# First attention of an eight-sublayer kernel: head maxima of the first two groups in eight PSUM banks, later batches projected between maxima, layer norms cut into pieces

## The chip, the cores and the metric

One Trainium2 chip, one of its cores. The core has five engines that run their own instruction streams and wait for each other by semaphores: TensorE (PE in the profile; its weight loads are PEld), VectorE (DVE), ScalarE (ACT), GpSimd (POOL) and SyncE (SP), which here issues transfers. The metric is the device time of one launch in microseconds (us); less is better.

## The reference

The input `x` has 4 sequences of 512 tokens of 128 features. Eight sublayers follow, each `x = x + f(layernorm(x))`: attention A, experts, attention B, experts, then four more of another kind. The change touches the first sublayer, attention A, and the layer norm of the second. Attention A is causal softmax attention with 16 heads of 8 features. The reference goes over key blocks with a running maximum, which is the same as subtracting each row's maximum over all allowed keys:

```python
def proj(W):
    y = jnp.einsum('btm,nm->btn', x, W)
    return y.reshape(Bx, Tx, N_HEADS, D_HEAD).transpose(0, 2, 1, 3)
Q, K, V = (proj(Wq), proj(Wk), proj(Wv))
...
scores = scale * jnp.einsum('bhtd,bhsd->bhts', Q, kb)
scores = jnp.where(future[None, None], -jnp.inf, scores)
m_new = jnp.maximum(m, jnp.max(scores, axis=-1, keepdims=True))
p = jnp.exp(scores - m_new)
...
return acc / jnp.maximum(l, 1e-12)
```

The layer norm ahead of each sublayer is `(x - m) / jnp.sqrt(v + 1e-5)` over the 128 features.

## The kernel before

Every engine has a function of its own for each sublayer, and the order of its calls, written out by hand, is the order of that engine's instructions. Nothing is reordered afterwards. PSUM is used as eight banks of 128 x 512 f32 (`bank(M, b)`); `take` makes PE wait until the last reader of a bank is done.

**The work of attention A.** A batch is one sequence (four, b = 0 to 3). A group n is four heads of one batch, so there are 16 groups and n // 4 is the batch. For each group the kernel does the following. *Maxima*: PE computes the scores of a 128-row tile of queries against the keys up to it, adds the causal mask by one more matmul, and DVE reduces them to a row maximum (`maxima`/`reduce`, 11 jobs of 384 or 512 columns a group, in the two side banks 6 and 7 in turn). *Split and rows*: DVE splits the maxima into three bf16 parts (`maxima_split`), PE transposes them (`rows`), DVE copies them (`row_copy`) and SP puts them as extra rows beside the queries, so that the second pass of scores comes out with the maximum subtracted. *Exps*: PE computes the transposed scores (`exps`, `tail`), ACT takes the exponential into `a_PT`, GpSimd zeroes what the mask forbids (`seen`). *Values*: PE multiplies them with the values and with a column of ones (`values`), ACT copies the result (`evict`), PE turns it (`turned`), and DVE divides (`normalize`). In the loop over n = 2 to 15, PE works on the maxima of group n + 2, the exponentials of group n and the values of group n - 1, woven together.

**Where queries and keys come from.** For groups 2 to 15 PE projects a batch (`factor`, q and k), ACT copies the result to `a_f`, which is split into three bf16 parts of `a_parts` by four steps (`split`: cast, subtract, cast, subtract) on GpSimd, except the keys of batch 0, which DVE splits. SP writes the parts to HBM (`write`) and reads them back spread over partitions (`read(n)`). A `read(n)` is 0.58 MB in four transfers, and those of groups 4 to 7 wait until batch 1 is written. Groups 0 and 1 of batch 0 are handled without that trip: PE projects them anew in a layout with one head in each block of 32 partitions (`own`), and their maxima (`own_maxima`, `own_reduce`), rows (`own_rows`, `own_add`) and exponentials (`own_exps`) use f32 matmuls on 32 rows, four heads at a time. The maxima of such a group come in three parts, by tiles of queries: `A_FIRST = [[3], [0, 2], [1]]`, of 512, 128 + 384 and 256 columns a head. They use banks 4 to 7, one a head, so that a part's matmuls wait until DVE has reduced the part before.

**The norms.** `norm_front` (DVE: statistics of four tiles, their aggregates, the variance), `norm_root` (GpSimd: the power -1/2), `norm_back` (DVE: one Newton step of four small operations, then four scalings into `XN`), then PE's `turn_tensor` and ACT's `turn_scalar` into `XNT`. Norm 0 is that of attention A; all four batches' fronts are at the start, and the backs of batches 1, 2 and 3 stand among the first maxima. Norm 1 is that of the experts: batch b - 1 gets its residual in group n = 4b + 2 (n = 6, 10, 14), and its norm follows there and in the next group. `expert_bias` is a preparation for the experts on DVE, in the group n = 14.

## Time and profile before

| | |
|---|---|
| median of 3 runs | 1227.47 us (1222.32 to 1230.30) |
| profiled execution: its time, its span | 1233.54 us, 1231.8 us |
| attention A in the span | 0 to about 250 us |
| busy in the whole span | PE 81%, DVE 68%, ACT 32%, POOL 28% |
| mean granted TensorE clock | 0.875 of full |

The profile is of one execution. A timeline row gives start, length, engine, line and operation, what it writes and reads, the count of instructions merged, and in brackets the idle time of the engine before it with what ended it; a "+" of neighbours on one line is merged, so a row can hold short waits. The granted clock of TensorE is 1.00 (2.4 GHz) or 0.50 (1.2 GHz); values between are stretches with both.

### The profile page before, as it was taken

The page shows a single profiled execution, that of the slowest core. Times are in us where ns is not written, and L with a number is a line of the kernel's source. Part 1 is how long each engine was busy: PE and PEld are TensorE (multiplying, and loading weights), DVE is VectorE, ACT ScalarE, POOL GpSimd, SP SyncE. Part 2 cuts the span into 40 slices and gives each one's busy share as a digit, 9 for nine tenths or more (in the row PEclk, how much of TensorE's full clock was granted, in tenths as well). Part 3 has the DMA queues.
Part 4 walks back from the last instruction along what each step waited for, and adds up shares of the span by engine and source line. Part 5 has one row for each costly group of instructions (what it writes and reads, how often), then busy time and mean ns, then how long its engine had stood idle before and what let it go on. Part 6 is the DMA issues. An engine that isn't in the chain of part 4 may idle for free.

```text
span 1231.8 us, 16801 instructions
## 1 busy us (share of the span) xinstructions
PE 1001.3 (81%) x6199; PEld 589.5 (48%) x6199; DVE 838.8 (68%) x1999; ACT 388.7 (32%) x650; POOL 345.2 (28%) x350
## 2 busy tenths in 40 slices
PE   6799899789999877699789754999999565997475
PEld 3334444334343655444334322766777344776244
DVE  7578787566554567766765476747655996588895
ACT  2335454523433243323323262221212122331121
POOL 5442222212233443212222303022020343232232
PEclk9889898989999687889889886999999796887786
DMA  5532121020000000000000000000000000000000
GB/s 136 146 104 60 40 60 61 32 89 1 1 1 1 1 1 1 1 0 1 1 0 1 1 0 3 1 1 1 1 1 1 1 1 1 2 2 2 0 10 26
DMA packets 11534, 24.35 MB, mean 20 GB/s; under 512 B 1323, under 2 KB 7635, under 8 KB 11315
## 3 DMA queue, kind: packets, MB, share of 16 engines
q1 hardware_dynamic: 11152, 22.28, 6.1%
...
## 4 chain that ended last, share of the span: by engine, by line
PE 55%; DVE 32%; issue 6%; ACT 3%; POOL 2%; DMA 1%; DVEq 0%; ACTq 0%; SPq 0%; POOLq 0%
PE ps L880 5%; PE ps L867 4%; PE ps L872 4%; PE ps L308 3%; PE ps L258 3%; DVE a_MN L462 2%; DVE XN L117 2%; DVE q_E L1501 2%; PE ps L1701 2%; PE ps L1762 2%; PE ps L1716 2%; PE ps L1759 2%; PE ps L278 2%; PE ps L2292 2%; DVE g_C L1637 1%
## 5 line engine op out<-in xcount | busy, mean ns | idle before, releaser
L1124 POOL TENSOR_TENSOR f_Y<-f_Y,f_TT 128x512 f32<-128x512 f32 x56 | 70.9, 1266 | 181.0 <-DVE f_TT L1014 181.0
L462 DVE TENSOR_REDUCE a_MN<-ps 128x1 f32<-128x384 f32 (+3 forms) x154 | 94.9, 639 | 35.0 <-PE ps L261 33.2
L1089 ACT ACTIVATE f_HH<-ps,pack_zero 128x512 f32<-128x512 f32 x64 | 44.0, 688 | 135.3 <-PE ps L867 135.2
L96 POOL TENSOR_TENSOR rs<-t,mhalf 128x4 f32<-128x4 f32 x37 | 37.5, 1015 | 175.3 <-DVE t L90 175.1
L143 DVE TENSOR_TENSOR X<-ps,X 128x512 f32<-128x512 f32 x32 | 22.0, 688 | 93.9 <-PE ps L1772 49.5
L597 ACT ACTIVATE a_PT<-ps 128x1024 f32<-128x1024 f32 x56 | 57.4, 1025 | 75.1 <-PE ps L278 73.9
L880 PE MATMUL ps<-f_HH,pack_zero 128*128 128x512 f32 x128 | 75.5, 673 | 5.7 <-DVE f_TT L1014 5.7
L1005 DVE TENSOR_TENSOR f_XS<-ps,XNT 128x512 f32<-128x512 f32 x64 | 43.9, 689 | 51.6 <-PE ps L860 51.5
L867 PE MATMUL ps<-f_XS,pack_zero 128*128 128x512 f32 x128 | 70.7, 636 | 1.1 <-DVE f_XS L1005 1.1
L258 PE MATMUL ps<-a_KS,a_QS 72*128 72x128 bf16 (+3 forms) x224 | 59.5, 326 | 13.1 <-DVE a_MN L462 7.5
L1014 DVE SCALAR_TENSOR_TENSOR f_TT<-ps,pack_zero,f_X 128x512 f32<-128x512 f32 x64 | 47.9, 748 | 32.0 <-PE ps L880 31.9
L872 PE MATMUL ps<-f_XS,pack_zero 128*128 128x512 f32 x128 | 68.7, 619 | 0.0
L2115 PE MATMUL ps<-pack_one,XNT 128*128 128x352 f32 x128 | 49.9, 538 | 22.6 <-DVE q_HH L2164 22.3
L688 POOL TENSOR_SCALAR_AFFINE_SELECT a_PT<-a_PT 128x256 f32<-128x256 f32 x64 | 26.0, 407 | 119.0 <-ACT a_PT L597 111.2
L2134 PE MATMUL ps<-pack_one,q_HT 128*128 128x128 f32 (+1 forms) x192 | 36.1, 334 | 20.9 <-ACT q_HT L2217 20.9
L308 PE MATMUL ps<-a_PT,a_VA 128*32 128x128 f32 (+3 forms) x512 | 51.1, 472 | 2.2 <-POOL a_PT L691 2.1
L258 PEld LDWEIGHTS ps<-a_KS,a_QS 72*128 72x128 bf16 x224 | 19.1, 102 | 62.6 <-DVE a_MN L462 41.5
L1093 ACT ACTIVATE f_X<-ps 128x512 f32<-128x512 f32 x64 | 38.2, 597 | 32.8 <-PE ps L873 32.8
L2115 PEld LDWEIGHTS ps<-pack_one,XNT 128*128 128x128 f32 x128 | 27.2, 225 | 40.3 <-DVE q_HH L2164 26.6
L278 PE MATMUL ps<-a_QS,a_KS 75*128 75x512 bf16 (+1 forms) x224 | 46.3, 313 | 0.0
L2134 PEld LDWEIGHTS ps<-pack_one,q_HT 128*128 128x128 f32 (+1 forms) x192 | 29.3, 228 | 30.2 <-ACT q_HT L2217 23.2
L1959 POOL TENSOR_TENSOR h_RN<-h_N,mhalf 128x32 f32<-128x32 f32 x4 | 21.7, 5433 | 76.3 <-DVE h_N L1818 76.3
...
## 6 DMA issues: line engine op xcount, KB each, us to landing
...
X<-in_x SPq DMA_DIRECT2D x4, 256.0 KB, 10.1
...
a_QS<-a_MT SPq DMA_DIRECT2D x42, 4.0 KB
```

Source lines behind the costliest of these rows:

```text
L258: pe.matmul(bank(M, bk, N, N * u), M.a_QS[0:72, i, h, 128 * ti:128 * ti + 128], M.a_KS[0:72, i, h, 0:N], start=(u == 0), stop=False, skip_ ...
L278: return pe.matmul(out, M.a_KS[0:75, i, h, 128 * si:128 * si + 128], M.a_QS[0:75, i, h, 128 * si:512], start=True, stop=True)
L308: m = pe.matmul(bank(M, 5, N, 128 * si, 32 * j, 32 * j + 32), M.a_VA[:, i, si, 4 * g + j, :], M.a_PT[:, (4 * n + j) % 8, A_AT[si]:A_AT[si] ...
L462: dve.tensor_reduce(M.a_MN[:, n % 2, ti, h0:h0 + k], bank(M, M.bank["a_max", n, jj], 128 * (ti + 1) * k).rearrange("p (a c) -> p a c", a=k ...
L597: act.activation(M.a_PT[:, c % 8, 0:1024], M.ps[:, a * 512:a * 512 + 1024], ACT.Exp).then_inc(made.sem, made.tick(n, hh))
L867: pe.matmul(bank(M, 2 + u % 2), M.f_w1[:, e, :], M.f_XS[:, x, :], start=True, stop=True).then_inc(made.sem, made.tick(n, u, 1))
L872: pe.matmul(bank(M, 4), M.f_w3[:, e, :], M.f_XS[:, x, :], start=True, stop=False)
L880: pe.matmul(bank(M, 5), M.f_w2[:, e, :], M.f_HH[:, u % 3, :], start=True, stop=True).then_inc(made.sem, made.tick(n, u))
L1014: dve.scalar_tensor_tensor(M.f_TT[:, u % 3, :], bank(M, 5), M.f_b2[:, e:e + 1], M.f_X3[:, u % 3, :], ALU.add, ALU.mult).then_inc(made.sem, ...
L1124: pool.tensor_tensor(M.f_Y[:, i, :], M.f_Y[:, i, :], M.f_TT[:, u % 3, :], ALU.add).then_inc(made.sem, made.tick(n, u))
L2115: pe.matmul(bank(M, 2 * k + s, 352), M.XNT[:, 128 * t:128 * t + 128], M.WG[:, s, :], start=True, stop=True).then_inc(made.sem, made.tick(n ...
L2134: m = pe.matmul(bank(M, bo, 128, 128 * (t % 4)), M.q_HT[0:rows, t % 2, a, :], M.WD[0:rows, a, :], start=(a == 0), stop=(a == 2))
```

## The change

- The first maxima: `own_maxima` gets the first bank and the number of heads that it takes at a time. Group 0 puts its first part in banks 4 to 7, its second in banks 0 to 3, its third in banks 4 to 7 two heads at a time; group 1 uses banks 4 to 7, the later two parts two heads at a time.
- What stood among these maxima is moved behind them: `own(1)` behind the rows of group 0, batch 1's turning and `factor` behind the maxima of group 1, `plain(0)` behind that; batch 2's turning and `factor` stand between the maxima of group 2, batch 3's between those of group 3. ACT, DVE and GpSimd follow the same order.
- Batch 0's keys are split on GpSimd, ahead of batch 1's, and no longer on DVE.
- DVE: all twelve `own_reduce` of group 0 come first, then `own_add`, then norm 0's back of batch 1; those of batches 2 and 3 come behind group 1's rows and behind `reduce(3, 1)`.
- Norm 1 of batches 0 to 2 is cut up: statistics, aggregates, Newton step and scalings stand between the reduces of the group with g = 3, one group boundary later than before. GpSimd's root for it stands ahead of that group's `seen` instead of behind the previous group's, which is the same place in its own order.

```diff
-    own_maxima(0, 0)
-    own(1, "q", 1)
-    own(1, "k", 2)
-    plain(0, 3)
-    own_maxima(0, 1)
+    own_maxima(0, 0, 4, 4)
+    own_maxima(0, 1, 0, 4)
+    own_maxima(0, 2, 4, 2)
+    own_rows(0, 6)
+    own(1, "q", 4)
+    own(1, "k", 5)
+    own_exps(0, 0)
+    own_maxima(1, 0, 4, 4)
+    own_exps(0, 1)
+    own_maxima(1, 1, 4, 2)
+    own_exps(0, 2)
+    own_maxima(1, 2, 4, 2)
     turn_tensor(pe, S, M, 0, 1, 0, M.XN, (S["normed"], (0, 1)))
+    own_rows(1, 4)
     factor(1, "q", 1)
     factor(1, "k", 2)
-    own_maxima(0, 2)
-    own_rows(0, 3)
-    own_exps(0, 0)
-    own_maxima(1, 0)
...
+    plain(0, 3)
     pe.wait_ge(S["in_ones"].sem, 16)
     own_exps(1, 0)
-    for jj in range(4):
+    maxima(2, 0)
+    maxima(2, 1)
+    turn_tensor(pe, S, M, 0, 2, 4, M.XN, (S["normed"], (0, 2)))
+    maxima(2, 2)
+    maxima(2, 3)
+    factor(2, "q", 4)
+    maxima(2, 4)
+    factor(2, "k", 5)
+    own_exps(1, 1)
+    for jj in range(5, 9):
         maxima(2, jj)
     values(0, 0)
...
     values(0, 3)
+    maxima(3, 1)
     turn_tensor(pe, S, M, 0, 3, 0, M.XN, (S["normed"], (0, 3)))
+    maxima(3, 2)
+    maxima(3, 3)
     factor(3, "q", 1)
+    maxima(3, 4)
     factor(3, "k", 2)
+    maxima(3, 5)
+    rows(2)
     plain(1, 3)
```

```diff
     for n in range(2, 16):
         b, g, more = n // 4, n % 4, n + 2 < 16
-        if more:
-            for jj in range(5):
+        left = b - 1 if g == 3 and b else None
+        for jj in range(5):
+            if more:
                 reduce(n + 2, jj)
+            if left is not None and jj < 2:
+                norm_stats(dve, S, M, left, M.X, range(2 * jj, 2 * jj + 2))
+            if left is not None and jj == 2:
+                norm_mean(dve, S, M, 1, left)
         if n + 1 < 16:
             row_copy(n + 1)
         if more:
             reduce(n + 2, 5)
-        if g == 3 and b:
-            norm_back(dve, S, M, 1, b - 1, M.X, M.XN)
+        if left is not None:
+            norm_refine(dve, S, M, 1, left)
+        if more:
+            reduce(n + 2, 6)
+        if left is not None:
+            norm_scale(dve, S, M, 1, left, M.X, M.XN, range(0, 2))
         normalize(n - 2)
...
-        if g == 2 and b:
-            norm_front(dve, S, M, 1, b - 1, M.X)
         if n == 14:
             expert_bias(dve, S, M)
```

```diff
     for b in range(4):
         norm_root(pool, S, M, 0, b)
-    split(0, "q")
-    split(1, "q")
-    split(1, "k")
+    for b in range(2):
+        split(b, "q")
+        split(b, "k")
```

**PE at the start.** L208 and L215 (after: L229 and L236) are the first maxima and their mask, `a_QS` holding the queries and keys of groups 0 and 1; L185/L204 is `own(1)`, L193 `plain`, L127 the turning, L177 `factor`, L226/L247 `own_rows`, L262 `own_exps`. Before, from the first maxima of group 0 to its rows:

```order
L208 MATMUL ps<-a_QS 128x512 x4
L215 MATMUL ps<-pack_half 128x128 x4
L185 MATMUL ps<-XNT,pack_first 128x512 x2
L193 MATMUL ps<-pack_first,XNT 128x128 x4
L208 MATMUL ps<-a_QS 128x128 x4
L208 MATMUL ps<-a_QS 128x384 x4
L215 MATMUL ps<-pack_half 128x2x128 x4
L127 MATMUL ps<-pack_first,XN 128x128 x4
L177 MATMUL ps<-XNT,pack_first 128x512 x2
L208 MATMUL ps<-a_QS 128x256 x4
L215 MATMUL ps<-pack_half 128x128 x4
L226 MATMUL ps<-pack_first,a_OL 128x128 x4
```

The same stretch of the change:

```order
L229 MATMUL ps<-a_QS 128x512 x4
L236 MATMUL ps<-pack_half 128x128 x4
L229 MATMUL ps<-a_QS 128x128 x4
L229 MATMUL ps<-a_QS 128x384 x4
L236 MATMUL ps<-pack_half 128x2x128 x4
L229 MATMUL ps<-a_QS 128x256 x2
L236 MATMUL ps<-pack_half 128x128 x2
L229 MATMUL ps<-a_QS 128x256 x2
L236 MATMUL ps<-pack_half 128x128 x2
L247 MATMUL ps<-pack_first,a_OL 128x128 x4
L204 MATMUL ps<-XNT,pack_first 128x512 x2
```

Between the first maxima and the rows of group 0 nothing is left but maxima; the projections and the turning stand behind.

**DVE at the boundary of group n = 6 and in group n = 7.** L462/L478 is a reduce, L85/L84 to L90/L94 the front of norm 1 for batch 0, L101 (L110) the first step of its back, L477/L493 the last step of a maxima split, L484/L500 `row_copy`. Before, from the end of the split in group 6:

```order
L477 TENSOR_TENSOR a_M<-a_MR,a_M 128x4x4
L85 BN_STATS st<-X 128x6 x4
L88 BN_AGGR mv<-st 128x2 x4
L90 TENSOR_SCALAR t<-mv 128x4
L462 TENSOR_REDUCE a_MN<-ps 128x4
L462 TENSOR_REDUCE a_MN<-ps 128x2 x2
L462 TENSOR_REDUCE a_MN<-ps 128x1 x2
L484 COPY a_MT<-ps 12x512
L462 TENSOR_REDUCE a_MN<-ps 128x1
L101 TENSOR_TENSOR t<-rs 128x4
```

The same stretch of the change:

```order
L493 TENSOR_TENSOR a_M<-a_MR,a_M 128x4x4
L478 TENSOR_REDUCE a_MN<-ps 128x4
L84 BN_STATS st<-X 128x6 x2
L478 TENSOR_REDUCE a_MN<-ps 128x2
L84 BN_STATS st<-X 128x6 x2
L478 TENSOR_REDUCE a_MN<-ps 128x2
L92 BN_AGGR mv<-st 128x2 x4
L94 TENSOR_SCALAR t<-mv 128x4
L478 TENSOR_REDUCE a_MN<-ps 128x1 x2
L500 COPY a_MT<-ps 12x512
L478 TENSOR_REDUCE a_MN<-ps 128x1
L110 TENSOR_TENSOR t<-rs 128x4
```

The front stood in one piece ahead of the first reduce; it is now between the first four reduces. Of the back, which follows, the diff shows that one reduce now comes ahead of the scalings, and that two of them stand behind the division.

**DVE at the end of the loop, n = 14 and 15**, where no maxima are left. L819/L839 is the end of `expert_bias`. Before:

```order
L85 BN_STATS st<-X 128x6 x4
L88 BN_AGGR mv<-st 128x2 x4
L90 TENSOR_SCALAR t<-mv 128x4
L805 CAST f_hb<-pack_zero 48x128
L807 TENSOR_TENSOR f_r<-pack_zero,f_hb 48x128
L809 CAST f_mb<-f_r 48x128
L811 TENSOR_TENSOR f_r<-f_r,f_mb 48x128
L812 TENSOR_SCALAR f_hi<-f_hb,pack_zero 48x128
L814 SCALAR_TENSOR_TENSOR f_mid<-f_mb,pack_zero,f_hi 48x128
L816 SCALAR_TENSOR_TENSOR f_r<-f_r,pack_zero,f_mid 48x128
L819 TENSOR_SCALAR f_B<-f_r,pack_zero 48x128 x8
L101 TENSOR_TENSOR t<-rs 128x4
```

The same stretch of the change:

```order
L836 SCALAR_TENSOR_TENSOR f_r<-f_r,pack_zero,f_mid 48x128
L839 TENSOR_SCALAR f_B<-f_r,pack_zero 48x128 x8
L84 BN_STATS st<-X 128x6 x4
L92 BN_AGGR mv<-st 128x2 x4
L94 TENSOR_SCALAR t<-mv 128x4
L110 TENSOR_TENSOR t<-rs 128x4
L112 TENSOR_TENSOR t<-t 128x4
L114 TENSOR_SCALAR t<-t 128x4
L116 TENSOR_TENSOR rs<-rs,t 128x4
```

The statistics of batch 2 stood ahead of `expert_bias`, with GpSimd's root beside it; they are now behind it, directly ahead of the Newton step.

## Rows read from the trace of the kernel before

**Rows 1.** The profile page: span; the chain that ended last, by engine

```profile
span 1231.8 us, 16801 instructions
...
PE 55%; DVE 32%; issue 6%; ACT 3%; POOL 2%; DMA 1%; DVEq 0%; ACTq 0%; SPq 0%; POOLq 0%
```

**Rows 2.** The chain of waits that ended last: start, length, what

```profile
28.00 2.65 DVE XN L117 x3
```

**Rows 3.** Timeline of the first maxima on PE and DVE, and GpSimd's splits beside them

```profile
14.53 1.14 PE L208 MATMUL ps<-a_QS 32*128 32x512 f32 x8
...
15.80 2.92 DVE L117 TENSOR_SCALAR XN<-X,mv,rs 128x128 f32<-128x128 f32 x4
...
18.64 2.47 DVE L448 TENSOR_REDUCE a_OL<-ps 128x1 f32<-128x512 f32 x4
...
23.27 2.74 DVE L448 TENSOR_REDUCE a_OL<-ps 128x1 f32<-128x128 f32 x8
...
26.14 0.61 POOL L673 CAST a_parts<-a_f 128x512 bf16<-128x512 f32 x1 [6.27 <-ACT a_f L571]
...
27.01 3.64 DVE L117 TENSOR_SCALAR XN<-X,mv,rs 128x128 f32<-128x128 f32 x4
...
32.12 1.09 PE L226 MATMUL ps<-pack_first,a_OL 128*128 128x128 f32 x4 [4.82 <-DVE a_OL L448]
...
32.56 1.15 POOL L679 TENSOR_TENSOR a_parts<-a_rest,a_parts 128x512 bf16<-128x512 f32 x1
...
34.20 2.09 PE L241 MATMUL ps<-a_QS 32*128 32x512 f32 x8 [0.99 <-DVE a_QS L456]
```

**Rows 4.** Timeline: one `factor` of q and k; `read(4)`; first exponentials of groups 2 and 3

```profile
24.28 1.96 PE L177 MATMUL ps<-XNT,pack_first 128*128 128x512 f32 x4 [0.78 <-ACT XNT L135]
...
39.84 0.31 SPq L723 DMA_DIRECT2D a_QS<-scratch  x1
...
76.31 1.06 PE L278 MATMUL ps<-a_QS,a_KS 75*128 75x512 bf16 x3
...
88.48 0.60 PE L278 MATMUL ps<-a_QS,a_KS 75*128 75x512 bf16 x3
```

**Rows 5.** Stretches: length, busy PE, PEld, DVE, ACT, POOL (instructions), granted clock, DMA share, GB/s

```profile
20.00:22.00 2.00, 0.63 (x13) 0.56 (x16) 1.97 (x4) 0.00 (x0) 0.00 (x0) 1.00 0.59 198
...
30.00:32.00 2.00, 0.00 (x0) 0.00 (x0) 1.98 (x5) 0.00 (x0) 1.86 (x3) 0.59 0.88 195
...
71.70:81.40 9.70, 9.50 (x39) 3.09 (x37) 6.54 (x15) 1.02 (x1) 3.02 (x4) 0.50 0.50 165
```

**Rows 6.** The same view over four stretches from one group's values to the next's

```profile
88.50:98.60 10.10, 9.70 (x85) 4.26 (x84) 8.68 (x20) 5.58 (x9) 2.95 (x7) 1.00 0.22 72
...
132.30:148.20 15.90, 12.70 (x92) 5.82 (x95) 12.61 (x39) 6.61 (x9) 3.88 (x7) 0.84 0.14 38
...
148.20:159.00 10.80, 10.40 (x84) 4.29 (x83) 8.02 (x18) 5.25 (x8) 2.93 (x6) 0.92 0.22 57
...
182.00:198.80 16.80, 13.67 (x91) 6.16 (x87) 12.38 (x38) 6.34 (x9) 3.89 (x7) 0.76 0.16 56
```

**Rows 7.** Timeline of group 7: norm front, GpSimd's root, PE's two waits for DVE

```profile
132.56 0.86 DVE L85 BATCH_NORM_STATS2 st<-X 128x6 f32<-128x128 f32 x4
...
133.99 1.01 POOL L96 TENSOR_TENSOR rs<-t,mhalf 128x4 f32<-128x4 f32 x1 [1.80 <-DVE t L90]
...
134.56 0.39 PE L258 MATMUL ps<-a_KS,a_QS 72*128 72x256 bf16 x2 [1.15 <-DVE a_MN L462]
...
140.91 0.39 PE L258 MATMUL ps<-a_KS,a_QS 72*128 72x512 bf16 x1 [1.68 <-DVE a_f L497]
```

**Rows 8.** Timeline of groups 14 and 15 on DVE and PE

```profile
230.56 2.20 DVE L819 TENSOR_SCALAR f_B<-f_r,pack_zero 48x128 bf16<-48x128 f32 x8
...
233.47 1.32 DVE L117 TENSOR_SCALAR XN<-X,mv,rs 128x128 f32<-128x128 f32 x4
...
237.39 2.36 PE L308 MATMUL ps<-a_PT,a_VA 128*32 128x512 f32 x32
```

More of the change, by code:

```diff
@@ L447, in own_reduce @@
             N = 128 * (ti + 1)
-            m = dve.tensor_reduce(M.a_MX[:, n, ti, 32 * j + 8:32 * j + 9], bank(M, 4 + j, N, at), AXX, ALU.max, negate=True)
+            m = dve.tensor_reduce(M.a_MX[:, n, ti, 32 * j + 8:32 * j + 9], bank(M, M.bank["a_max", n, part, j], N, at), AXX, ALU.max, negate=True)
             at += N
@@ L505, in attn_a_vector @@
         norm_front(dve, S, M, 0, b, M.X)
+    for part in range(3):
+        for j in range(4):
+            own_reduce(0, part, j)
+    own_add(0)
     norm_back(dve, S, M, 0, 1, M.X, M.XN)
-    for j in range(4):
-        own_reduce(0, 0, j)
-    split("k")
-    for j in range(4):
-        own_reduce(0, 1, j)
-    norm_back(dve, S, M, 0, 2, M.X, M.XN)
-    for j in range(4):
-        own_reduce(0, 2, j)
-    own_add(0)
     for part in range(3):
@@ L523, in attn_a_vector @@
     maxima_split(2)
-    for jj in range(6):
+    reduce(3, 0)
+    reduce(3, 1)
+    norm_back(dve, S, M, 0, 3, M.X, M.XN)
+    for jj in range(2, 6):
         reduce(3, jj)
@@ L538, in attn_a_vector @@
             reduce(n + 2, 5)
-        if g == 3 and b:
-            norm_back(dve, S, M, 1, b - 1, M.X, M.XN)
+        if left is not None:
[4 more added lines that the diff above has]
+            norm_scale(dve, S, M, 1, left, M.X, M.XN, range(0, 2))
         normalize(n - 2)
         if more:
-            for jj in range(6, 9):
-                reduce(n + 2, jj)
+            reduce(n + 2, 7)
+        if left is not None:
+            norm_scale(dve, S, M, 1, left, M.X, M.XN, range(2, 4))
+        if more:
+            reduce(n + 2, 8)
         if g == 2 and b:
@@ L547, in attn_a_vector @@
         if more:
-            for jj in range(9, 11):
-                reduce(n + 2, jj)
+            reduce(n + 2, 9)
+            reduce(n + 2, 10)
             maxima_split(n + 2)
-        if g == 2 and b:
-            norm_front(dve, S, M, 1, b - 1, M.X)
         if n == 14:
@@ L633, in attn_a_scalar @@
     own(1)
-    plain(0)
+    for part in range(3):
+        own_exps(0, part)
     turn_scalar(act, S, M, 0, 1)
     factors(1)
-    for part in range(3):
-        own_exps(0, part)
+    plain(0)
+    own_exps(1, 0)
     turn_scalar(act, S, M, 0, 2)
     factors(2)
-    for part in range(3):
-        own_exps(1, part)
+    own_exps(1, 1)
+    own_exps(1, 2)
     turn_scalar(act, S, M, 0, 3)
```

112 lines of the change are left out of this document (48 added, 64 removed).

## Prediction

> **What bounds the kernel now.** I read the page first: the span, and the chain that ended last, which is 55% PE and 32% DVE [rows 1]. No engine is full; the two hand work to each other, so a microsecond counts where one waits for the other. Attention A is some 250 us of the span and the only part that the change touches, so I went through it by the chain of waits, the timeline and stretches with the granted clock. Three places matter.
>
> *The start.* The first maxima run at 14.53, and group 0's exponentials start only at 34.20 [rows 3]. DVE is what they wait for: batch 1's norm back (2.92), four reduces (2.47), the keys' split, eight reduces (2.74), batch 2's norm back (3.64), and then the last four. The second norm back is in the chain of waits [rows 2], and PE stands still 4.82 us until 32.12 for what follows it [rows 3]. The clock falls in that gap: the stretch 30 to 32 has 0.59, while 20 to 22, after a shorter gap, has 1.00 [rows 5]. Group 2's exponentials come at 76.31, in a cold stretch (0.50 from 71.7 to 81.4, PE busy 9.50 of 9.70), and group 3's at 88.48 [rows 4, 5]. A warm group takes 10.10 with PE busy 9.70: PE sets that pace, DVE has 1.4 to spare [rows 6].
>
> *Groups 7 and 11.* They hold norm 1 and take 15.90 and 16.80, with DVE busy 12.61 and 12.38 and a mean clock of 0.84 and 0.76; the group behind the first takes 10.80 [rows 6]. PE waits 1.15 for the front and 1.68 for the back [rows 7], and then the clock falls.
>
> *The end.* In groups 14 and 15 DVE does `expert_bias` to 232.76, then the last norm back to 234.79; PE's turning, ACT's copy and the last values (237.39) follow [rows 8].
>
> **The change, part by part.** The sum is made against the profiled 1233.5 us. The median is 6.1 lower, 1227.5; I carry the difference over.
>
> *A. To group 0's exponentials.* DVE's first reduce can start when mask and fronts are done, about 15.8, where the old norm back started. Now nothing is between the reduces: 2.47 + 2.74 + 1.47 (from 30.65, the end of the norm back, to PE's 32.12) = 6.7, to 22.5. PE always has the next part ready, since the second is in free banks and the third needs only four reduces. The rows and the addition took 2.08 (32.12 to 34.20) at the low clock; with the 1.09 of transposes halved it is 1.5. PE meanwhile does `own(1)`, as large as the `factor` of 1.96 [rows 4]: 22.5 + 0.7 + 2.0 = 25.2 is the start of the exponentials, against 34.20: 9.0 less.
>
> *B. From there to group 2's exponentials.* Group 1's maxima start at 26.4 behind 1.1 of exponentials' matmuls. Their twelve reduces again cost 6.7, plus 0.4 where PE waits for ACT to give banks back: 27.8 to 34.8. Then on PE rows 0.7, `factor` 2.0, `plain` 1.0 (half of `factor`'s), hand-over and ACT's copy 0.9: 39.5. One part of exponentials, and DVE's first reduce of group 2 comes at 41.2. Group 2's eleven maxima would take 7; `factor(2)`, two parts of exponentials and two of values stand between them on PE and make it 12, to 53.2. DVE's split 1.0, two reduces 1.3 (2.47 is four), batch 3's norm back 2.0 (232.76 to 234.79 in [rows 8]): 57.5. Turning and ACT's copy 1.3, nine reduces, the row copy and the waits for `factor(3)` 7.6: 66.4. So group 2's exponentials start at 66.5 instead of 76.31: **9.8 less**. Before, this way held less of projections (they lay under DVE's work), which is why it gains hardly more than A.
>
> *What the move puts elsewhere.* Batch 0's key split leaves DVE and costs GpSimd one split: two took 26.14 to 33.71, so 3.8 [rows 3]. It ends at 23.7, where DVE's was done before 23.27, so group 2's copies from HBM come no later. Batch 1's splits now start at 37.5 rather than 26.1; GpSimd then has splits, `seen(0)` (3.0, GpSimd's 2.95 of a group [rows 6]), splits, `seen(1)`, splits in a row. `seen(0)` ends at 48.1, and PE wants it at 48.8: covered by 0.7. SP's `read(4)` to `read(7)` wait for the write of batch 1 and go at 47.7 instead of 39.84 [rows 4]; 2.3 MB at the 165 GB/s of a stretch full of writes [rows 5] are 14 us, so the last lands by 62, and PE asks for the first at 66. The norm backs of batches 1 and 2 lie where DVE waits for PE anyway (from 24.1 and from 36.4; the latter may be stretched like the 2.92 and 3.64 by GpSimd's splits, to 40): nothing.
>
> *C. The group after.* From group 2's exponentials to group 3's took 12.17 [rows 4], a warm group 10.10 [rows 6]: 5.1 of cold clock cost 2.1. **2.1 less** if it is warm.
>
> *D. The price of new gaps.* PE is idle 19.0 to 22.6 (its maxima are done, DVE is not) and 55.0 to 57.5 (for batch 3's norm back). The old gap of 4.82 brought the clock down, the one ahead of 21.37 (2.7) did not; 3.6 and 2.5 are between and below. A fall costs something like the 2.1 of C; with the chain half on DVE, I take 0 to 3 each and **2.5 more** for one of two.
>
> Here the skill speaks against the change. The Trainium skill, "TensorE: Matmul & The Clock Gate", section "HAM oscillation — how this bites in real kernels", says that a matmul stream with waits between its bursts is throttled again at each and starts every burst cold, and reckons the penalty at half of the throttled time. By it the 5.1 us of C would cost 2.55, where the rows have 2.1. No row shows whether a gap of 3.6 brings a fall.
>
> *E. Groups 7 and 11.* DVE's work is the same, 12.6; only its order changes. Its front is 1.43 from statistics to the root's start [rows 7]. In pieces, PE's first wait of 1.15 becomes waits of 0.45, 0.25 and 0.4 behind each piece. The long one stays: PE wants the side bank that `normalize` frees, and ahead of that DVE had Newton step, four scalings and division, and has now Newton step, a reduce, two scalings and division. Two scalings are exchanged for one reduce, 0.6 each, so the 1.68 stays. From DVE's split to its next, counted through, it is 13.1 after 13.2: as good as nothing at the same clock. What can be had is the cold clock: a group of 14.0 instead of 15.90 and 16.80, and 10.1 instead of 10.8 behind it: 2.6 and 3.5. PE's idle time falls from 3.2 (15.90 less 12.70) to about 2.5 a group, so I take it for one of the two: **3 less**. The ends are +0.5 (more small waits, nothing warm) and 6.1 less.
>
> *F. The end.* In n = 14 the statistics stood ahead of `expert_bias` and GpSimd's root beside it. Now all is in a row: `expert_bias` ends 1.3 earlier, at 231.5, then 1.43 of front, 1.0 of root, 0.1 of hand-over, 0.7 of Newton step, and 1.3 of scalings with a division of 0.7 between them: 236.7 instead of 234.79. PE turns, ACT copies and only then evicts group 14, so the last values move from 237.39 to 239.3: **1.9 more**. GpSimd's root also stands ahead of group 15's `seen`, which ends at 237.1 and is covered. From here everything is serial and moves along.
>
> Sum: -9.8 - 2.1 + 2.5 - 3.0 + 1.9 = -10.5: 1223 for a profiled run, **1217** for the median.
>
> **The rivals.** *All warm.* No new gap brings the clock down, and both norm groups keep it: -9.8 - 2.1 - 6.1 + 1.9 = -16.1, **1211**. For it: the 2.7 gap did not matter. Against: the 1.68 wait stays, and both such groups have a mean clock well below 1.
>
> *Cold as ever.* The rule of the skill cited above: both gaps of the start cost 2.5, and the norm groups gain nothing: -9.8 - 2.1 + 5 + 0.5 + 1.9 = -4.5, **1223**. For it: PE's bursts at the start are about 3 us between waits.
>
> *The start is held by GpSimd and the transfers.* Batch 1's splits are 11 later and their user is 10 earlier; the margins are 0.7 for `seen(0)` and a few us for the reads. If `seen` is slower beside DVE, or the transfers are, the group 2 chain stands at about 73: 3 instead of 9.8 won, **1224**. In the extreme, the change does not do what it says: 1227.
>
> *Slower.* The clock falls in the first new gap and, as small gaps follow each other, does not rise before group 2's exponentials. In 71.7 to 81.4 it stayed low 9.7 us with PE busy 98%, so work alone does not raise it at once. PE has about 27 of warm work between 22.6 and 66.5, 54 when cold, in 44: more than 10 late, which eats A and B, and F stays: **1230**. It decides from some 30 us of unbroken cold; that stretch of 9.7 is the longest that I can point to.
>
> **How the numbers follow.** Chances: forecast 0.39, all warm 0.24, cold as ever 0.23, GpSimd and transfers 0.10, slower 0.04. About 1%, 12.3 us, is what a measurement of this kernel can tell from no change; the three runs before lie 8 apart. Faster by more than 1% means below 1215.2: nearly all of the warm case and a quarter of the forecast's own, 1212 to 1221, make 0.33; slower by over 1% 0.02; the rest 0.65. The range takes in the warm and the cold case with their bounds: 1209 to 1226.
>
> **What the changed profile would show.** Group 0's first exponentials' matmuls at 25 (A); group 2's at 66 to 69 (B); group 3's 10.1 behind (C); the granted clock in 20 to 24 and 56 to 62 (D); group 7 at 14 or at 16, with PE's wait of 1.7 behind the division in both (E); DVE's last scalings ahead of the last values later than `expert_bias` by 5, not by 2 (F). I am wrong if group 2's maxima wait for their copies, if GpSimd ends `seen(0)` after PE asks for it, or if the clock stays up in the norm groups although the wait remains.

## The result, and the profile after

| | before | changed |
|---|---|---|
| median (range) | 1228.88 us (1222.32 to 1231.57), 4 runs | 1247.86 us (1246.15 to 1251.64), 4 runs |
| profiled execution, its span | 1233.54, 1231.8 | 1251.64, 1249.8 |
| mean granted clock | 0.875 | 0.864 |

The ratio is 1.0167, with a 95% interval of 1.0119 to 1.0214. It is estimated from all runs of both kernels, so it is not exactly the quotient of the two medians. The whole interval is above 1: the kernel is slower, and the forecast of 1217 was wrong in sign.

The two lines of the page that say most are those of the costliest groups for DVE's reduces and PE's maxima. In the kernel before they are:

```profile
L462 DVE TENSOR_REDUCE a_MN<-ps 128x1 f32<-128x384 f32 (+3 forms) x154 | 94.9, 639 | 35.0 <-PE ps L261 33.2
...
L258 PE MATMUL ps<-a_KS,a_QS 72*128 72x128 bf16 (+3 forms) x224 | 59.5, 326 | 13.1 <-DVE a_MN L462 7.5
```

The page of the changed kernel:

```profile
span 1249.8 us, 16805 instructions
...
PE 58%; DVE 30%; issue 6%; ACT 3%; POOL 2%; DMA 0%; DVEq 0%; ACTq 0%; POOLq 0%
...
L478 DVE TENSOR_REDUCE a_MN<-ps 128x1 f32<-128x384 f32 (+3 forms) x154 | 95.0, 640 | 48.5 <-PE ps L282 47.9
...
L279 PE MATMUL ps<-a_KS,a_QS 72*128 72x128 bf16 (+3 forms) x224 | 60.3, 330 | 19.4 <-DVE a_f L513 12.4
```

The reduces are as many and as long as before (154, 95 us), but DVE now waits 48.5 us ahead of them instead of 35.0. PE waits 19.4 us ahead of its maxima instead of 13.1, and the first cause has changed: not a reduce (`a_MN`) but `a_f` of L513, the last step of the division in `normalize`. Nothing in the forecast accounts for that.

One warm group without a norm shows why. Stretches of the changed kernel, with the columns of [rows 5]:

```profile
98.20:109.30 11.10, 9.79 (x83) 4.23 (x83) 8.72 (x20) 5.53 (x8) 2.94 (x6) 1.00 0.42 103
...
133.50:151.20 17.70, 14.93 (x97) 6.63 (x97) 13.05 (x40) 7.04 (x10) 4.35 (x8) 0.76 0.13 32
```

The first is such a group, at full clock: 11.10 instead of 10.10 [rows 6], with the same work for PE (9.79 and 9.70) and DVE (8.72 and 8.68). The second is group 7 with 0.7 of the group ahead of it, at a mean clock of 0.76. The middle of the first, in the timeline, is:

```profile
101.54 0.41 DVE L500 COPY a_MT<-ps 12x512 bf16<-12x512 bf16 x1
...
102.45 0.56 DVE L478 TENSOR_REDUCE a_MN<-ps 128x1 f32<-128x384 f32 x1 [0.49 <-PE ps L282]
...
103.06 0.34 PE L279 MATMUL ps<-a_KS,a_QS 72*128 72x384 bf16 x1 [0.21 <-DVE a_MN L478]
...
103.49 0.56 DVE L478 TENSOR_REDUCE a_MN<-ps 128x1 f32<-128x384 f32 x1 [0.49 <-PE ps L282]
...
103.97 0.16 DVE L509 TENSOR_SCALAR a_RS<-ps 128x16 f32<-128x16 f32 x1
...
104.45 0.29 DVE L513 TENSOR_TENSOR a_f<-ps,a_RS 128x128 f32<-128x128 f32 x1
...
104.80 0.39 PE L279 MATMUL ps<-a_KS,a_QS 72*128 72x512 bf16 x1 [0.91 <-DVE a_f L513]
```

The same place in the kernel before:

```profile
93.66 0.56 DVE L462 TENSOR_REDUCE a_MN<-ps 128x1 f32<-128x384 f32 x1 [0.49 <-PE ps L261]
...
94.14 0.16 DVE L493 TENSOR_SCALAR a_RS<-ps 128x16 f32<-128x16 f32 x1
...
94.62 0.29 DVE L497 TENSOR_TENSOR a_f<-ps,a_RS 128x128 f32<-128x128 f32 x1
94.83 1.32 DVE L462 TENSOR_REDUCE a_MN<-ps 128x1 f32<-128x384 f32 x2
...
94.97 0.39 PE L258 MATMUL ps<-a_KS,a_QS 72*128 72x512 bf16 x1
```

PE's job 7 of the maxima (the first of 512 columns) needs the side bank that the division frees. Before, DVE divided directly behind its reduce of job 5, while PE computed job 6. Now `reduce(n + 2, 6)` stands ahead of `normalize(n - 2)`, so DVE first waits 0.49 for job 6's matmuls, then reduces them, then divides. From the reduce of job 5 to PE's job 7 it takes 104.80 - 102.45 = 2.35 instead of 94.97 - 93.66 = 1.31: **1.04 more in a group**. The diff has this swap outside every condition on `left`; it holds in all twelve groups that have maxima to reduce (n = 2 to 13), not only in the two of them with a norm.

**Where the time went.** The two profiled executions, stage by stage:

| stretch | before | changed | difference |
|---|---|---|---|
| group 2's exponentials start | 76.31 | 70.68 | -5.6 |
| values of group 1 start | 77.94 | 72.08 | -5.9 |
| from there, groups 2 to 13 | 142.00 | 156.21 | +14.2, of it 12 x 1.04 = 12.5 |
| groups 14 and 15 | 17.45 | 22.07 | +4.6, of it 3.25 in the last |
| the last values start | 237.39 | 250.36 | +13.0 |
| batch 3's scalings of norm 1 | 249.15 | 265.31 | +16.2 |
| span | 1231.8 | 1249.8 | +18.0 |

The last values' 32 matmuls alone took 2.36 [rows 8] before and 4.50 now, at the low clock; that is 2.1 of the 3.2 between the last values and batch 3's scalings. I call the start of those scalings **the mark** below: it ends attention A, and no kernel here changes anything behind it.

**The end**, in the timeline of the changed kernel:

```profile
239.23 1.65 DVE L839 TENSOR_SCALAR f_B<-f_r,pack_zero 48x128 bf16<-48x128 f32 x8
...
242.36 1.01 POOL L105 TENSOR_TENSOR rs<-t,mhalf 128x4 f32<-128x4 f32 x1 [4.00 <-DVE t L94]
...
244.15 0.57 DVE L114 TENSOR_SCALAR t<-t 128x4 f32<-128x4 f32 x1
...
245.11 0.99 DVE L131 TENSOR_SCALAR XN<-X,mv,rs 128x128 f32<-128x128 f32 x2
...
246.71 0.60 DVE L131 TENSOR_SCALAR XN<-X,mv,rs 128x128 f32<-128x128 f32 x2
247.45 0.63 PE L146 MATMUL ps<-pack_first,XN 128*128 128x128 f32 x4 [3.64 <-DVE XN L131]
...
250.36 4.50 PE L329 MATMUL ps<-a_PT,a_VA 128*32 128x512 f32 x32
```

PE stands still 3.64 us for the scalings, and the clock is down when the last values start.

**The start.** Stretches of the changed kernel around its two new gaps, and PE's and DVE's rows there:

```profile
20.00:22.00 2.00, 0.00 (x0) 0.00 (x0) 2.00 (x7) 0.00 (x0) 1.85 (x3) 1.00 0.33 107
22.00:24.00 2.00, 1.24 (x5) 0.92 (x6) 1.06 (x3) 0.00 (x0) 1.86 (x3) 0.78 1.03 342
24.00:26.00 2.00, 2.00 (x4) 0.67 (x2) 1.86 (x9) 0.69 (x1) 0.24 (x1) 0.50 0.86 288
...
58.00:60.00 2.00, 0.00 (x0) 0.00 (x0) 1.90 (x5) 0.00 (x0) 2.00 (x5) 0.50 0.78 174
```

```profile
22.76 0.76 PE L247 MATMUL ps<-pack_first,a_OL 128*128 128x128 f32 x4 [3.06 <-DVE a_OL L464]
23.31 3.49 PE L204 MATMUL ps<-XNT,pack_first 128*128 128x512 f32 x4
26.73 1.14 PE L262 MATMUL ps<-a_QS 32*128 32x512 f32 x8
...
54.37 1.04 DVE L487 CAST a_M<-a_MN 128x16 bf16<-128x16 f32 x1
...
58.24 0.57 DVE L114 TENSOR_SCALAR t<-t 128x4 f32<-128x4 f32 x1
...
59.20 1.50 DVE L131 TENSOR_SCALAR XN<-X,mv,rs 128x128 f32<-128x128 f32 x4
60.84 1.09 PE L146 MATMUL ps<-pack_first,XN 128*128 128x128 f32 x4 [5.65 <-DVE XN L131]
...
70.68 0.82 PE L299 MATMUL ps<-a_QS,a_KS 75*128 75x512 bf16 x3
```

The clock fell in the second gap and directly behind the first, so twice and not once. Behind the first, `own(1)` took 3.49 instead of about 2.0. The second was 5.65 long, not 2.5.

### The profile page after: what moved, and what is told of

Read it like the earlier page. It is cut to its first block, busy times and chain, and to the rows that moved or that the text cites. A ratio compares the mean times of both kernels' runs of the same rounds, so it can differ in the third digit from the quotient of the medians.

```text
span 1249.8 us, 16805 instructions
## 1 busy us (share of the span) xinstructions
PE 1017.0 (81%) x6199; PEld 603.2 (48%) x6199; DVE 841.8 (67%) x1995; ACT 389.4 (31%) x650; POOL 348.6 (28%) x354
## 4 chain that ended last, share of the span: by engine, by line
PE 58%; DVE 30%; issue 6%; ACT 3%; POOL 2%; DMA 0%; DVEq 0%; ACTq 0%; POOLq 0%
PE ps L900 5%; PE ps L887 4%; PE ps L892 4%; PE ps L329 3%; PE ps L279 3%; DVE a_MN L478 3%; PE ps L2312 2%; PE ps L1782 2%; DVE XN L131 2%; PE ps L1721 2%; PE ps L1736 2%; PE ps L1779 2%; DVE q_E L1521 2%; PE ps L299 1%; DVE g_C L1657 1%
## 5 line engine op out<-in xcount | busy, mean ns | idle before, releaser
L478 DVE TENSOR_REDUCE a_MN<-ps 128x1 f32<-128x384 f32 (+3 forms) x154 | 95.0, 640 | 48.5 <-PE ps L282 47.9
L900 PE MATMUL ps<-f_HH,pack_zero 128*128 128x512 f32 x128 | 73.0, 652 | 5.7 <-DVE f_TT L1034 5.7
L279 PE MATMUL ps<-a_KS,a_QS 72*128 72x128 bf16 (+3 forms) x224 | 60.3, 330 | 19.4 <-DVE a_f L513 12.4
L887 PE MATMUL ps<-f_XS,pack_zero 128*128 128x512 f32 x128 | 68.6, 619 | 1.3 <-DVE f_XS L1025 1.3
L892 PE MATMUL ps<-f_XS,pack_zero 128*128 128x512 f32 x128 | 67.5, 610 | 0.0
L329 PE MATMUL ps<-a_PT,a_VA 128*32 128x128 f32 (+3 forms) x512 | 55.4, 509 | 1.4 <-POOL a_PT L714 1.3
L299 PE MATMUL ps<-a_QS,a_KS 75*128 75x512 bf16 (+1 forms) x224 | 48.8, 326 | 0.1
```

The costliest lines, as they stand in the source:

```text
L279: pe.matmul(bank(M, bk, N, N * u), M.a_QS[0:72, i, h, 128 * ti:128 * ti + 128], M.a_KS[0:72, i, h, 0:N], start=(u == 0), stop=False, skip_ ...
L299: return pe.matmul(out, M.a_KS[0:75, i, h, 128 * si:128 * si + 128], M.a_QS[0:75, i, h, 128 * si:512], start=True, stop=True)
L329: m = pe.matmul(bank(M, 5, N, 128 * si, 32 * j, 32 * j + 32), M.a_VA[:, i, si, 4 * g + j, :], M.a_PT[:, (4 * n + j) % 8, A_AT[si]:A_AT[si] ...
L478: dve.tensor_reduce(M.a_MN[:, n % 2, ti, h0:h0 + k], bank(M, M.bank["a_max", n, jj], 128 * (ti + 1) * k).rearrange("p (a c) -> p a c", a=k ...
L887: pe.matmul(bank(M, 2 + u % 2), M.f_w1[:, e, :], M.f_XS[:, x, :], start=True, stop=True).then_inc(made.sem, made.tick(n, u, 1))
L892: pe.matmul(bank(M, 4), M.f_w3[:, e, :], M.f_XS[:, x, :], start=True, stop=False)
```

## The experiments

"Division" is `normalize(n - 2)`, "job k" is the k-th part of a group's maxima and its reduce. The mark and the group lengths come from one profiled execution each, a group's length being the time from the start of the values of the group ahead of it to that of its own. The ratios are against the kernel before, run beside it on the same chip: its median was 1234.72 beside e1 to e4, 1231.88 beside e5 to e8 and 1230.58 beside e9 and e10.

| kernel | median us | ratio to before, 95% | mark | group 7, group 11, last group |
|---|---|---|---|---|
| before | | | 249.15 | 15.81, 16.92, 8.61 |
| changed | 1247.86 | 1.0167 (1.0119 to 1.0214) | 265.31 | 16.97, 16.27, 11.86 |
| e1_r6_back | 1232.41 | 1.0001 (0.9972 to 1.0031) | 243.56 | 13.02, 15.73, 12.31 |
| e2_r6_only | 1244.89 | 1.0078 (1.0053 to 1.0102) | 266.60 | 17.67, 17.57, 9.08 |
| e3_start_only | 1230.75 | 0.9979 (0.9954 to 1.0003) | 242.76 | 15.95, 17.24, 8.62 |
| e4_pieces_only | 1236.04 | 1.0022 (0.9994 to 1.0050) | 250.75 | 13.02, 15.57, 12.31 |
| e5_end_as_before | 1226.26 | 0.9970 (0.9942 to 0.9997) | 239.59 | 13.02, 16.22, 8.61 |
| e6_divide_first | 1220.01 | 0.9913 (0.9882 to 0.9944) | 237.00 | 12.57, 12.56, 8.61 |
| e7_gap_filled | 1219.56 | 0.9903 (0.9873 to 0.9933) | 234.61 | 12.56, 12.57, 8.61 |
| e8_back3_early | 1216.01 | 0.9870 (0.9843 to 0.9897) | 236.03 | 12.57, 12.56, 8.61 |
| e9_changed_again | 1245.35 | 1.0108 (1.0051 to 1.0165) | 262.24 | 16.94, 16.28, 11.86 |
| e10_before_divide_first | 1233.42 | 1.0030 (0.9998 to 1.0062) | 249.09 | 14.74, 17.59, 10.20 |

**e1: only job 6 put back behind the division**, in all groups; the rest of the change stays.

```diff
-        if more:
-            reduce(n + 2, 6)
         if left is not None:
             norm_scale(dve, S, M, 1, left, M.X, M.XN, range(0, 2))
         normalize(n - 2)
         if more:
+            reduce(n + 2, 6)
             reduce(n + 2, 7)
```

> The changed kernel, but in every group of the loop DVE divides first and reduces job 6 behind it, as before the change. Theory 1 (DVE's division, which frees a side bank for PE, comes later by one reduce in each of the twelve groups with maxima, at 1.0 us a group): the loop goes back to 10.1 us a warm group, 12 us less than the changed kernel, so 0.990 to 0.997 of the kernel before (the start gains 5.6, the end loses 3 to 5, the clock in the last values 2). Theory 2 (the loop is slow because the new start leaves GpSimd, the copies and the clock in another state): it stays at 1.016 and a group at 11.1.

Groups 3, 4 and 13 are back at 10.08, and the slowdown is gone: ratio 1.0001 (0.9972 to 1.0031). The gain of 0.3 to 1% over the kernel before, which I expected as well, did not come. In groups 2 to 13 e1 takes 137.2 where the changed kernel took 156.2 (153.5 in its second profile, e9), 16 to 19 more. So beside the 12.5 that the swap costs directly, the changed kernel lost 4 to 6.5 there, in groups that it ran in part at the low clock and e1 did not. On the page, DVE's wait ahead of its reduces falls from 48.5 to 30.9, PE's ahead of its maxima from 19.4 to 9.6, and the first cause is a reduce again:

```profile
L478 DVE TENSOR_REDUCE a_MN<-ps 128x1 f32<-128x384 f32 (+3 forms) x154 | 94.5, 638 | 30.9 <-PE ps L282 29.5
...
L279 PE MATMUL ps<-a_KS,a_QS 72*128 72x128 bf16 (+3 forms) x224 | 57.8, 317 | 9.6 <-DVE a_MN L478 5.6
```

**e2: only job 6 ahead of the division**, in the kernel before.

```diff
+        if more:
+            reduce(n + 2, 6)
         normalize(n - 2)
         if more:
-            for jj in range(6, 9):
+            for jj in range(7, 9):
                 reduce(n + 2, jj)
```

> The kernel before with one edit: in every group of the loop DVE reduces job 6 ahead of the division, not behind it. Theory 1: a warm group takes 11.1 instead of 10.1 and the whole 12 us more, 1.010 of the kernel before. Theory 2: no change, 0.998 to 1.002.

This one swap costs 0.78% (0.53 to 1.02), 9.6 us, and makes warm groups of 11.13. Groups 2 to 13 take 157.6 instead of 142.0 in its profile, again more than 12.5. Its page has the changed kernel's signature:

```profile
L462 DVE TENSOR_REDUCE a_MN<-ps 128x1 f32<-128x384 f32 (+3 forms) x154 | 95.2, 640 | 49.3 <-PE ps L261 48.5
...
L258 PE MATMUL ps<-a_KS,a_QS 72*128 72x128 bf16 (+3 forms) x224 | 61.0, 333 | 23.0 <-DVE a_f L497 13.4
```

Put in alone, the swap makes the kernel slower by 0.78%; taken out alone, it takes away the 1.08 to 1.67% that the changed kernel loses (e9 and the first comparison). That settles the cause of the sign. The sizes do not quite add up: with the swap out, the rest of the change makes no difference (e1), so the other 0.3 to 0.9% would arise only where both are together; for e9's 1.08% the intervals overlap, and it may be nothing. The traces show such time in groups 7, 8 and 13, which the changed kernel runs in part at the low clock and e1 does not. That this is all of it is not shown.

**e3: the new start with DVE's loop of before**, so that norm 1 is in two pieces at its old places and job 6 behind the division.

```diff
 # DVE, for n in range(2, 16): as before the change
+        if g == 3 and b:
+            norm_back(dve, S, M, 1, b - 1, M.X, M.XN)
         normalize(n - 2)
...
+        if g == 2 and b:
+            norm_front(dve, S, M, 1, b - 1, M.X)
```

> The start of the changed kernel with DVE's loop of the kernel before (norm 1 in one piece at its old place, division ahead of job 6). Theory 1: group 2's exponentials at 70.7 and 10.1 a group from there, so 4 to 6 us less than the kernel before, 0.995 to 0.997. Theory 2: 1.00 or more, since the late splits and copies slow the groups behind them.

Group 2's exponentials start at 70.65, 5.7 earlier than before, and the mark is 6.4 earlier. The median shows 0.2% less (at most 0.46%), which can't be told from nothing.

**e4: the pieces of norm 1 with the old start**, job 6 behind the division.

```diff
 # the kernel before, with DVE's loop of e1:
+            if left is not None and jj < 2:
+                norm_stats(dve, S, M, left, M.X, range(2 * jj, 2 * jj + 2))
+            if left is not None and jj == 2:
+                norm_mean(dve, S, M, 1, left)
```

> The start of the kernel before with the norms of the loop in pieces, the division ahead of job 6. Theory 1: the pieces alone gain nothing in groups 7 and 11 (15.5 to 16 each) and cost 2 to 3 us at the end, where they stand behind the experts' bias: 1.001 to 1.003. If the pieces were what costs, it would be 1.01 or more.

Groups 7, 8, 11 and 12 take 13.02 + 10.08 + 15.57 + 11.56 = 50.2 instead of 15.81 + 10.89 + 16.92 + 11.16 = 54.8, so the pieces gain 4.5 there. The last group takes 12.31 instead of 8.61, which gives 3.7 back, and the last values' 32 matmuls take 3.33 instead of 2.36. The whole can't be told from nothing: +0.22% (-0.06 to +0.50). I had expected 15.5 to 16 for groups 7 and 11; group 11 took that and group 7 did not. PE's three longest waits are the same in both (0.44, 0.33 and 1.17), and so they are in e1 and e5, but in all three kernels group 7 keeps the full clock and group 11 loses it behind the wait of 1.17. Here are both in e5:

```profile
127.00:140.00 13.00, 10.47 (x88) 4.65 (x87) 11.86 (x39) 5.98 (x9) 3.79 (x7) 1.00 0.07 16
...
172.80:189.10 16.30, 14.00 (x92) 6.28 (x95) 12.41 (x39) 6.54 (x9) 3.80 (x7) 0.76 0.18 57
```

**e5: e1 with batch 2's norm as before**, its statistics ahead of `expert_bias` in n = 14 and its back in one piece at n = 15.

```diff
-        left = b - 1 if g == 3 and b else None
+        left = b - 1 if g == 3 and 0 < b < 3 else None
...
+        if n == 15:
+            norm_back(dve, S, M, 1, 2, M.X, M.XN)
         normalize(n - 2)
...
         if n == 14:
+            norm_front(dve, S, M, 1, 2, M.X)
             expert_bias(dve, S, M)
```

> The changed kernel with the division ahead of job 6 (as e1), and with norm 1 of batch 2 as in the kernel before: statistics ahead of the experts' bias in n = 14, one back in n = 15. Theory (the pieces behind the bias delay the last norm, PE's turning, ACT's copy and the last values): from group 14's values to the last ones 8.6 us, not 12.3, and 3.7 us less than e1: 0.996 to 0.998 of the kernel before. Rival (the 12.3 is GpSimd's masks or the clock): it stays at 12.

The last group is 8.61 again, and the mark 4.0 earlier than in e1. The ratio, 0.9970 (0.9942 to 0.9997), is as expected and just clear of 1.

**e6: e5 with the division ahead of the norm's steps** in groups 7 and 11 too, and these further apart.

```diff
             reduce(n + 2, 5)
-        if left is not None:
-            norm_refine(dve, S, M, 1, left)
-            norm_scale(dve, S, M, 1, left, M.X, M.XN, range(0, 2))
         normalize(n - 2)
         if more:
             reduce(n + 2, 6)
+        if left is not None:
+            norm_refine(dve, S, M, 1, left)
+        if more:
             reduce(n + 2, 7)
         if left is not None:
-            norm_scale(dve, S, M, 1, left, M.X, M.XN, range(2, 4))
+            norm_scale(dve, S, M, 1, left, M.X, M.XN, range(0, 2))
         if more:
             reduce(n + 2, 8)
+        if left is not None:
+            norm_scale(dve, S, M, 1, left, M.X, M.XN, range(2, 4))
```

> As e5, and in groups 7 and 11 DVE divides directly behind job 5, ahead of the Newton step, whose result is needed only at the group's end. Theory (PE's wait of 1.6 is for the side bank that the division frees): the wait goes, both groups take about 12.5 us at full clock, 0.5 to 3 us each less than in e5. Rival (DVE's 12.6 of work sets the group whatever the order): no change, 13.0.

Both groups take 12.6 at full clock, and groups 3, 4, 8, 12 and 13 their warm 10.08. The stretches of groups 7 and 11 in e6:

```profile
126.80:139.40 12.60, 10.69 (x88) 4.66 (x87) 11.54 (x39) 6.09 (x9) 3.79 (x7) 1.00 0.08 21
172.20:184.80 12.60, 10.69 (x88) 4.66 (x87) 11.54 (x39) 6.10 (x9) 3.80 (x7) 1.00 0.22 74
```

PE's longest wait is now 0.46 in both. The ratio is 0.9913, and the whole interval is below 1. The edit moved the division forward and the norm's steps apart at once; which of the two did how much was not tried.

**e7: e6 with `own(1)` ahead of group 0's rows on PE**, in banks 0 and 1, to fill the first gap. **e8: e7 with batch 3's norm 0 back behind `reduce(2, 4)`**, to take it out of the second gap.

```diff
 # e7, PE
-    own_rows(0, 6)
-    own(1, "q", 4)
-    own(1, "k", 5)
+    own(1, "q", 0)
+    own(1, "k", 1)
+    own_rows(0, 6)
 # e8, DVE
-    for jj in range(11):
+    for jj in range(5):
+        reduce(2, jj)
+    norm_back(dve, S, M, 0, 3, M.X, M.XN)
+    for jj in range(5, 11):
         reduce(2, jj)
     maxima_split(2)
-    reduce(3, 0)
-    reduce(3, 1)
-    norm_back(dve, S, M, 0, 3, M.X, M.XN)
```

> As e6, and the projections of group 1 stand ahead of group 0's rows on PE, in banks 0 and 1, where PE otherwise stands still 3 us. Theory (the clock fell in that gap, and the projections were on the way to the exponentials): the clock stays at 1.00 to 28, group 0's exponentials start at 24.5, not 26.7, and 2 us less stay to the end. Rival (DVE and GpSimd set the pace behind it): earlier there, but nothing left at group 2's exponentials.

> As e7, and norm 0's back of batch 3 stands on DVE behind job 4 of group 2, where DVE waits for PE, and not behind job 1 of group 3. Theory (PE's idle 5.7 us ahead of batch 3's turning, with the clock falling in it, is the largest loss of the new start): the idle goes and group 2's exponentials come 4 to 6 us earlier, at 64 to 66. Rival (group 2 then waits for GpSimd, for its mask of group 1 or for copies): 1 or less.

In e7 the gap ahead of the rows shrank from 3.06 to 1.28, and group 0's exponentials started at 24.23 instead of 27.22. The clock still fell, later:

```profile
22.00:24.00 2.00, 0.63 (x4) 0.42 (x4) 1.19 (x4) 0.26 (x1) 1.85 (x3) 1.00 1.02 342
24.00:26.00 2.00, 1.77 (x12) 1.09 (x16) 1.86 (x9) 0.29 (x1) 0.32 (x1) 0.71 0.84 291
26.00:28.00 2.00, 2.00 (x16) 0.39 (x8) 0.35 (x2) 1.78 (x4) 0.00 (x0) 0.50 0.32 81
```

The mark moved 2.4, the median not measurably. The expected full clock up to 28 did not come. e8's profiled execution began its maxima 2.2 later than e7's (its `own(1)` starts at 21.68 instead of 19.50), and even so group 2's exponentials came 1.1 earlier (67.69 for 68.80), so the step itself gained 3.3, less than the 4 to 6 expected. Most of it was lost again at once: the clock was down from 67 to 77, and group 2 took 13.44 instead of 11.27. The mark is 1.4 later than in e7, so without the late start 0.8 of the 3.3 is left. e8 has the lowest median, 1216.01, and beats the kernel before by 1.30% (1.03 to 1.57). That it beats e6 and e7 is not shown: there are four runs of each, and they overlap.

**e9: the changed kernel once more**, unedited, to see how firm the size of the slowdown and of the group lengths is.

> The changed kernel once more, beside the kernel before on the same chip, and for its second profile. e1, e2 and e4 together say: division behind job 6 costs 1.05 in each of twelve groups, 12.6, and more where the clock falls in the wait that it makes; the end costs 3.7; the start gives 6. That is 10 to 16 us more than the kernel before, 1.009 to 1.017. If it comes out near 1.000, the first comparison was of another state of the chip and theory 1 is in doubt.

It is 1.08% slower this time (0.51 to 1.65), where the first comparison gave 1.67%; the intervals overlap. From group 4 on the group lengths repeat: groups 4 to 6 take 11.13, 12.09 and 12.75, and group 7 takes 16.94. Groups 2 and 3 do not: 12.32 and 11.12 here, 14.18 and 11.96 in the first profile, which has a stretch at the low clock from 81 to 88 that this one lacks (in 76 to 86 the mean clock is 1.00 here and 0.76 there).

**e10: the kernel before with division and job 6 ahead of the whole norm back** in groups 7, 11 and 15. It asks whether the place of the division alone makes e6's gain, or the cutting too.

```diff
+        normalize(n - 2)
+        if more:
+            reduce(n + 2, 6)
         if g == 3 and b:
             norm_back(dve, S, M, 1, b - 1, M.X, M.XN)
-        normalize(n - 2)
         if more:
-            for jj in range(6, 9):
+            for jj in range(7, 9):
                 reduce(n + 2, jj)
```

> The kernel before with one edit in groups 7, 11 and 15: DVE divides and reduces job 6 first, and the whole norm back (Newton step and four scalings) stands behind them. Theory (PE's wait of 1.7 ahead of job 7 is for the division alone): it gets shorter, the clock need not fall, and 1 to 6 us are won without any piece, 0.995 to 0.999. Rival (only the cut of the front and the back gets the groups to 12.6): they stay at 15.8 and 16.9, 0.999 to 1.001.

As a whole nothing is gained: 1.0030 (0.9998 to 1.0062) for the 0.995 to 0.999 expected. PE no longer waits for the division, but the front still costs it 1.15, and the undivided back now holds up the reduce of job 7, whose bank job 9 waits for. Group 7 is 1.1 shorter than before, group 11 is 0.7 longer, and the last group is 1.6 longer, since the edit was made there too. Group 7 in e10's timeline:

```profile
133.61 0.39 PE L258 MATMUL ps<-a_KS,a_QS 72*128 72x256 bf16 x2 [1.15 <-DVE a_MN L462]
...
139.26 1.20 DVE L117 TENSOR_SCALAR XN<-X,mv,rs 128x128 f32<-128x128 f32 x4
...
141.12 0.39 PE L258 MATMUL ps<-a_KS,a_QS 72*128 72x512 bf16 x1 [1.58 <-DVE a_MN L462]
...
143.29 1.11 PE L127 MATMUL ps<-pack_first,XN 128*128 128x128 f32 x4
```

The last row's 1.11 for four transposes is the low clock's time (0.63 at the high one, as at 247.45 above). The division early and the back whole give 14.74 and 17.59; the norm in pieces with the division behind them 13.0 and 15.6 to 16.2 (e1, e4, e5); both together 12.6 and 12.6 (e6).

## Why the prediction was wrong

**The step that failed is E.** It said: "Two scalings are exchanged for one reduce, 0.6 each, so the 1.68 stays", and looked at groups 7 and 11 only. Two errors are in it. The reduce of job 6 was read as part of the norm's new order, when the diff moves it ahead of the division for every n with maxima. And the reduce was priced as 0.6 of DVE work, when it first waits for matmuls (0.49) that PE has only just begun; PE in turn needs the bank that stands behind it. The swap costs 1.04 in each of twelve groups, 12.5 in all, and was not in the sum; in groups 2 to 13 as a whole it comes to 15.6 (e2 against the kernel before) and 16 to 19 (the changed kernel against e1), with the low clock that comes with it. e1 and e2 show it from both sides. The order of instructions of an ordinary group, which I didn't write out, would have shown it without a run; I wrote out only the two groups in which I expected something.

For groups 7 and 11 themselves E was right where it was narrow: PE's wait for the division stayed (1.64 for 1.68; 1.17 with job 6 back in its place) and the smaller ones came at 0.44, 0.15 and 0.33 for the 0.45, 0.25 and 0.4 given. With job 6 back in its place (e4) the gain was 4.5 over groups 7, 8, 11 and 12, against the 3 of the forecast, and as the forecast had it, one of the two groups kept the clock and the other did not. In the changed kernel it was not to be had: the two groups and those behind take 57.5 instead of 54.8, of which 4.2 is the swap, which leaves 1.5.

**A and B were right in kind and too large.** Group 0's exponentials started at 26.73 for 25.2: the gap was 3.06 for 3.6, but it brought the clock down, and `own(1)` took 1.5 more. Group 2's started at 70.68 for 66.5. Of the 2.7 lost between, the gap ahead of batch 3's turning is the clear part: 5.65 for 2.5. DVE's split began at 54.37 instead of 53.2 and was 0.9 longer, and the norm back took 3.3 (57.44 to 60.70) instead of 2.0. Five more profiles with this start and no further edit to it (e1, e3, e5, e6, e9) have 70.65 to 71.75, and the start of before, 76.31, came at 76.56, 77.77 and 75.35 in e2, e4 and e10. On the mean **5.4 is what the move gives, not 9.8** (or 7.3 with the fall of D), and in a median it can't be told from nothing (e3).

The longer steps on DVE have a visible partner. In the changed kernel's profile the third operation of the Newton step (L114) took 0.17 in each of the 31 cases in which GpSimd was idle, and 0.57 in the two in which GpSimd ran its mask. Each of these ended 0.02 to 0.03 behind the mask's instruction that had begun before it, and the first cast of the maxima split (1.04 instead of 0.22, at 54.37) ended as closely behind a subtraction of GpSimd's `split`:

```profile
54.22 1.16 POOL L698 TENSOR_TENSOR a_rest<-a_f,a_parts 128x512 f32<-128x512 f32 x1
...
58.15 0.64 POOL L714 TENSOR_SCALAR_AFFINE_SELECT a_PT<-a_PT 128x512 f32<-128x512 f32 x1
...
244.06 0.64 POOL L714 TENSOR_SCALAR_AFFINE_SELECT a_PT<-a_PT 128x512 f32<-128x512 f32 x1
```

So DVE seems to have waited inside these steps for GpSimd. The forecast allowed for this in the norm back of batch 2 ("may be stretched"), and not in that of batch 3 or in F, where the change put the steps beside GpSimd's masks and splits.

**C and D.** The next group was not warm. From group 2's exponentials to group 3's it took 12.17 before, 11.26 to 11.57 with the new start and job 6 in place (e1, e3, e5, e6), and 13.95 and 12.41 in the two profiles of the changed kernel, so C was worth 0.6 to 0.9 and not 2.1. In all of them the clock was down again for a few us from 71 to 72.5 on. The changed kernel's first profile has a further stretch at the low clock from 81 to 88, and the second has not, so that part is chance. D had given one fall at 2.5; there were two in the new gaps, and this third. The rival "cold as ever" had the two falls right. D also leaned on the old gap of 2.7, behind which the clock had stayed up; that was luck of one execution. In e4, whose start is that of before, the clock fell in the same gap:

```profile
21.78 2.04 PE L227 MATMUL ps<-a_QS 32*128 32x128 f32 x13 [2.72 <-DVE a_OL L467]
...
22.00:24.00 2.00, 2.00 (x18) 0.86 (x19) 1.70 (x3) 0.00 (x0) 0.00 (x0) 0.50 1.03 346
```

**F was right in sign and too small**: +1.9 forecast, +3.25 for the last group in the changed kernel and +3.7 in e4 and e1, and a further 1 to 2 for the last values at the low clock (not F's alone: e6 has 4.05 for them with the end as before). The mechanism is the one given, everything in a row behind `expert_bias`; from its end to the last scaling's it took 6.4 instead of 5.2. The Newton step was taken as 0.7 and took 1.7 (243.40 to 245.11). The delay shows as PE's wait of 3.64 ahead of the turning. What the term lacked altogether is the low clock behind it.

**The rivals.** GpSimd and the transfers did not hold the start: `seen(0)` ended at 49.74, ahead of the values at 50.27, and from 60.84 to 79.70 PE had no wait of 0.5 or more. "All warm" came true only in e6 to e8, and only for groups 7 and 11. The rival "slower" reached the right sign by a mechanism that did not occur: the clock was up again by 26.73, where group 0's first eight exponentials' matmuls took 1.14, as the first maxima did at full clock. With job 6 in place and nothing else changed, the kernel is the "within 1%" case that held 0.65 (e1), at 1.0001. So the one swap is why the sign was wrong, and even without it the forecast's gain of 10.5 was too large: A, B and D together had 7.3 for 5.4, C had 2.1 for less than 1, and F took 1.9 for 3.7 and more, where E had only 3 for 4.5.

**What stays open.** e1's and e3's marks are 5.6 and 6.4 earlier than before, while their medians show 0 and 2.6 less. e2's is 17.4 later, while its median shows 9.6 more; its profiled execution, 1250.01, is the slowest of its ten. The part behind the mark, the same work in every kernel, took 982.7 before, 987.2 in e1, 983.6 in e3 and 978.5 in e10 in their profiled executions, so a single execution can hide or feign such a difference. I can't say whether an early mark is partly lost later by cause or by chance.
